# W_dec over two queues, U over 128 rows, FFN's scale and offset on ScalarE: one change to a fused adaptive-norm and FFN kernel

## The reference

```
U = (mu @ W_dec + b_dec).reshape(B, IN_DIM + 1, K)      # B=128, mu 128x64, K=30
weight, bias = split(einsum('bik,kj->bij', U, V))
c = einsum('bsd,bde->bse', x, weight) + bias
gate = c @ Wg.T + bg; top 2 of 8, softmax
x = x + sum over the two of w * (gelu(c @ W1[e].T + b1[e]) @ W2[e].T + b2[e])

h = ln(x, pw_g[id], pw_b[id]); h = ln(h, cp_g[id2], cp_b[id2]); t, s likewise
z = mlp_ln(concat(w0*h, w1*t, w2*m, w3*n, w4*r, w5*s))  # last step: * int_g + int_be
f = silu(z @ w1) * (z @ w2); f = gelu(f @ h1); f = gelu(f @ h2)
x = x + f @ w3
```

## Time and profile before

| | us |
|---|---|
| median of 3 runs | 456.68 |
| lowest and highest | 456.17, 460.87 |
| the profiled execution | 454.07 |
| its span, first to last instruction | 452.2 |
| TensorE busy | 425.7 |
| VectorE busy | 328.6 |
| ScalarE busy | 278.7 |
| GpSimd busy | 141.2 |

### The profile page before, as it was taken

The page is one execution under the profiler, slowest core; times in us unless marked ns, Lnnn a source line. Parts: engine busy times, 40 slices in busy tenths (PEclk is TensorE's granted clock), DMA queues, the critical chain, the costliest instruction groups (busy, mean ns, idle before and its releaser), DMA issues.

```text
span 452.2 us, 5963 instructions
## 1 busy us (share of the span) xinstructions
PE 425.7 (94%) x1897; PEld 283.9 (63%) x1897; DVE 328.6 (73%) x693; ACT 278.7 (62%) x498; POOL 141.2 (31%) x135
## 2 busy tenths in 40 slices
PE   7998898799799999999999999999999999999696
PEld 3875554355366675676667766676577557777495
DVE  3459998699998587686785785887686696755633
ACT  1527836563775677567758665686568446676464
POOL 0013467716454078511011730372127111110000
PEclk9579989999999999999999999999999999999889
DMA  8962348226334027310511260045012400000001
GB/s 235 386 250 93 112 125 256 67 79 204 134 120 144 8 87 227 110 46 13 167 46 46 96 230 6 8 151 166 33 46 77 137 0 2 0 0 25 0 1 50
DMA packets 16847, 45.06 MB, mean 100 GB/s; under 512 B 3209, under 2 KB 5166, under 8 KB 16238
## 3 DMA queue, kind: packets, MB, share of 16 engines
q1 hardware_dynamic: 12240, 31.77, 21.4%
q0 software_dynamic: 3584, 10.49, 7.4%
q10 hardware_dynamic: 991, 2.40, 1.4%
HBM read 40.64 MB, written 4.03 MB: 99 GB/s over the span
## 4 chain that ended last, share of the span: by engine, by line
PE 68%; DVE 5%; ACT 4%; issue 2%; POOL 1%; POOLq 0%; ACTq 0%; DVEq 0%
PE bank L737 20%; PE bank L635 18%; PE bank L683 6%; PE bank L777 5%; PE bank L627 5%; PE bank L722 5%; PE bank L690 2%; PE bank L651 2%; PE bank L766 1%; POOL rstd L1421 1%; DVE bn L1163 1%; DVE mG L1153 1%; PE bank L678 1%; PE bank L696 1%; PE bank L646 1%
## 5 line engine op out<-in xcount | busy, mean ns | idle before, releaser
L635 PE MATMUL bank<-mG,W 128*128 128x512 f32 x256 | 120.8, 599 | 0.5 <-DVE mG L1153 0.5
L882 ACT ACTIVATE mG<-bank,keepP 128x512 f32<-128x512 f32 x128 | 85.9, 683 | 33.7 <-PE bank L627 27.0
L1421 POOL TENSOR_TENSOR rstd<-ve,mhalf 128x4 f32<-128x4 f32 x24 | 34.4, 1434 | 177.9 <-DVE ve L1169 177.1
L1153 DVE TENSOR_TENSOR mG<-mG,gwbs 128x1024 f32<-128x1024 f32 x64 | 78.9, 1240 | 1.9 <-DMA gwbs<-gate_w 1.6
L635 PEld LDWEIGHTS bank<-mG,W 128*128 128x128 f32 x256 | 47.5, 192 | 41.3 <-issue 36.8
L627 PE MATMUL bank<-ts,A 96*128 96x512 f32 x128 | 63.8, 533 | 6.8 <-ACT mG L882 5.0
L943 ACT ACTIVATE G<-bank,keepP 128x512 f32<-128x512 f32 x48 | 32.6, 690 | 26.1 <-PE bank L737 25.9
L1401 POOL DMA_INDIRECT gp<-pgb_in,ixall x32 | 39.9, 1247 | 22.4 <-DVE w_l L1069 11.6
L627 PEld LDWEIGHTS bank<-ts,A 96*128 96x128 f32 x128 | 24.0, 191 | 26.7 <-issue 12.6
L737 PE MATMUL bank<-hA_h,h1w_h 128*128 128x512 f32 x96 | 38.8, 404 | 0.0
L737 PE MATMUL bank<-hB_h,h2w_h 128*128 128x512 f32 x96 | 38.8, 404 | 0.0
(11 more groups left out here) (233 smaller groups left out, 844.8 us busy)
## 6 DMA issues: line engine op xcount, KB each, us to landing
gwbs<-gate_w SPq DMA_DIRECT2D x32, 512.0 KB
outT<-keep SPq DMA_DIRECT2D x7, 256.0 KB, 2.2
...
W1T<-W1T_in SPq DMA_DIRECT2D x1, 1024.0 KB, 10.0
W<-W2T_in SPq DMA_DIRECT2D x1, 1024.0 KB, 13.9
hs<-h1T_in SPq DMA_DIRECT2D x1, 1024.0 KB, 5.9
```

The source lines that it names most:

```text
L635: mm = pe.matmul(OACC[:, :], W2[:, e * HC + c, :], mG[n % NMG][:, c, :], start=False, stop=(e == E - 1 and c == HC - 1))
L882: act.activation(mG[e % NMG][:, c % HC, :], HM[n % 2][:, :], ACT.Gelu, bias=b1c[:, c:c + 1]).then_inc(m_gelu, 1)
L1153: dve.tensor_tensor(mG[n % NMG][:, :, :], mG[n % NMG][:, :, :], gwb[(n // 2) % 2][:, n % 2, :].unsqueeze(1).broadcast_to([P, HC, T]), ALU. ...
L1421: step(pool.tensor_tensor(rstd[:, n, :], ve[:, n, :], mhalf[:, :], ALU.pow))
```

## The change

- W_dec is loaded in two halves of 32 rows, one by SyncE's queue, one by ScalarE's. ScalarE issues all its early loads ahead of its first wait, and runs one tiny copy (`warmA`), so that its table is loaded then. `ld_wd` must reach 64.
- Of the eight pieces of `Wp`, VectorE copies six (0, 1, 2, 4, 6, 7) and ScalarE two (3, 5).
- `Wp` and `muT` have 128 rows. GpSimd clears rows 64 to 127 of the buffer under `Wp`, VectorE rows 64 to 127 of `muT`; row 64 is then filled. The U products, the one for the bias included, run over 128 rows. `WARM` is 5 in place of 6.
- `gap` is 512 values wider and `ct` is moved, so that block 0's gathered table rows (`gp0`) lie in the memory of W1T and `gap` alone, and `tab` of block 0 no longer waits for `small_src`.
- `ff` is a ScalarE instruction with the same scale and offset, and stands in ScalarE's order.
- All five orders are written anew; the FFN weights are split in another order (h2, w3, h1, w12), so that `tab` of block 1, which waits for the rest of w3, needs two of the four rests in place of four. The tables' first rows are shown, the other rows are left out.

```diff
         W1T = sb("W1T", [P, E * H], stack=early)
-        gap = sb("gap", [P, 6144 - KR * (D + 1) - E * H], stack=early)
+        gap = sb("gap", [P, 6656 - KR * (D + 1) - E * H], stack=early)
         VT3 = gap[:, 0:KA]
...
-        muT = sb("muT", [MU + 1, B], stack=early)
+        muT = sb("muT", [P, B], stack=early)
...
-        Wp = hs[0:MU + 1, 0:KR * (D + 1)].rearrange("m (k i) -> m k i", k=KR)
+        Wp = hs[:, 0:KR * (D + 1)].rearrange("m (k i) -> m k i", k=KR)
+        warmA = sb("warmA", [2, P], stack=early)
...
         gcm[0] = sb("gcm0", [P, TT, 3 * P])
-        ct = sb("ct", [P, T])
         gp[0] = sb("gp0", [P, TT, 2 * P])
         norms = sb("norms", [P, 4, TT, P])
         xh, tt, ss, hh = [norms[:, i, :, :] for i in range(4)]
-        cs_, ch = [sb(f"c{k}", [P, T]) for k in "sh"]
+        ct, cs_, ch = [sb(f"c{k}", [P, T]) for k in "tsh"]
...
-        wd_even, wd_odd = sems("wd_even", "wd_odd")
+        wd_dve, wd_act, wp_zero = sems("wd_dve", "wd_act", "wp_zero")
...
-        WARM = 6
+        WARM = 5
+        PIECES = ("v", "v", "v", "a", "v", "a", "v", "v")
...
         def weights_done(eng, *ns):
 
-            eng.wait_ge(w_lo, max((1, 2, 3, 4)[n] for n in ns))
+            eng.wait_ge(w_lo, max((4, 3, 1, 2)[n] for n in ns))
...
             "PE": (
-                (0, "tm0 tm1 gm0 sq0 A0 tm2 A1 tm3 A2 gx0 A3 sq1 tm4 H0 H1 gm1 H2 H3 H4 tm5 H5 H6 gm2 H7 B O0 H8 H9 O1 H10 gm3 sq2 "
-                    "tm6 gm4 H11 H12 O2 sq3 O3 H13 gx1 O4 H14 H15 O5"),
...
+                (0, "tm0 tm1 gm0 A0 A1 tm2 sq0 tm3 gm1 gx0 A2 A3 sq1 H0 H1 tm4 H2 H3 H4 tm5 gm2 H5 H6 tm6 H7 B H8 H9 O0 O1 sq2 gm3 "
+                    "H10 H11 sq3 gm4 O2 H12 gx1 H13 O3 H14 O4 H15"),
...
             "ACT": (
-                (0, "gh tch0 ah0 tch1 ah1 gth0 sza bh ah2 gxh0 gxc0 tch2 ah3 aw g0 g1 wh3 g2 g3 tch3 g4 g5 gth1 ws g6 g7 wh0 tch4 "
-                    "g8 wh1 g9 syc g10 g11 tch5 g12 g13 gxc1 smh0 g14 gxh1 g15"),
...
+                (0, "gh tch0 tch1 bh aw ah0 gth0 ah1 gxh0 sza gxc0 ah2 tch2 ah3 ws g0 g1 g2 g3 smh0 tch3 g4 g5 g6 g7 gth1 g8 tch4 "
+                    "g9 syc g10 g11 tch5 wh2 g12 g13 g14 gxc1 gxh1 smh1 smh2 g15"),
...
             "DVE": (
-                (0, "gl tb0 tb1 am top0 al0 sv0 tb2 gww0 bl al1 sv1 gxl0 tb3 al2 al3 sv3 sv2 top1 q0 gww1 tb4 q1 sv6 sv4 tb5 q2 wl0 "
-                    "q3 q4 tb6 q5 sv5 top2 q6 gxl1 q7 wl1 gww2"),
...
+                (0, "tb0 tb1 gl am top0 al0 gww0 sv0 tb2 tb3 al1 sv1 gxl0 bl al2 sv2 al3 top1 sv6 tb4 sv3 q0 q1 sv4 sml0 q2 tb5 q3 "
+                    "q4 sv5 gww1 top2 q5 gxl1 q6 q7 wl2 sml1 tb6 gww2 x"),
...
             "POOL": (
-                (0, "ix tcl0 tcl1 tcl2 tcl3 srt tcl4 tcl5 tab tcl6 rt0 tcl7 rt1"),
...
+                (0, "tcl0 tcl1 tcl2 srt tcl3 tcl4 tcl5 ix tab rt0 tcl6 rt1 tcl7"),
...
-            load(Wd[0:MU, :], A["W_dec"], ld_wd)
+            load(Wd[0:MU // 2, :], A["W_dec"][0:MU // 2, :], ld_wd)
...
-                if k % 8 == 0:
-                    pe.wait_ge(wd_even, k // 8 + 1)
-                elif k % 8 == 4:
-                    pe.wait_ge(wd_odd, k // 8 + 1)
+                if k % 4 == 0:
+                    who = PIECES[k // 4]
+                    pe.wait_ge(wd_dve if who == "v" else wd_act, PIECES[:k // 4 + 1].count(who))
...
+            def ff(b):
+                act.wait_ge(yT_mm, b + 1)
+                act.activation(flat(YN), XL[:, :], ACT.Identity, scale=igb[:, 0:1], bias=igb[:, 1:2]).then_inc(f_full, 1)
...
+            load(Wd[MU // 2:MU, :], A["W_dec"][MU // 2:MU, :], ld_wd)
             load(muT[0:MU, :], A["cond_512T"], ld_wd)
             load(Wd[MU:MU + 1, :], A["b_dec"], ld_wd)
+            load(Vk[:, :], A["V"], ld_v)
             load(keepP[:, :], A["keepP"], ld_v)
-            load(Vk[:, :], A["V"], ld_v)
-            act.wait_ge(setup0, 1)
-            act.wait_ge(ld_wd, 48)
             load(earlyP[:, :], A["earlyP"], ld_small)
-            wd = Wd[0:MU + 1, :].rearrange("m (i k) -> m k i", k=KR)
-            for q in range(1, 8, 2):
-                act.activation(Wp[:, 4 * q:min(4 * q + 4, KR), :], wd[:, 4 * q:min(4 * q + 4, KR), :], ACT.Copy).then_inc(wd_odd, 1)
             for b in (1, 2):
                 load(keep[b][:, :], A["xT"][:, b * T:(b + 1) * T], x_in[b])
             load(xTr[0][:, :], A["xT"][:, 3 * T:5 * T], ld_x[0])
             load(w12s[:, :], A["w12T"], ld_w[0])
+            act.wait_ge(setup0, 1)
+            act.activation(warmA[:, :], onesf[:, :], ACT.Copy)
+            act.wait_ge(ld_wd, 64)
+            act.wait_ge(wp_zero, 1)
+            wd = Wd[0:MU + 1, :].rearrange("m (i k) -> m k i", k=KR)
+            for q in range(8):
+                if PIECES[q] == "a":
+                    mine = slice(4 * q, min(4 * q + 4, KR))
+                    act.activation(Wp[0:MU + 1, mine, :], wd[:, mine, :], ACT.Copy).then_inc(wd_act, 1)
...
-                dve.wait_ge(w_hi, (2, 3, 4, 1)[n])
+                dve.wait_ge(w_hi, (4, 3, 1, 2)[n])
...
-            def ff(b):
-                dve.wait_ge(yT_mm, b + 1)
-                dve.tensor_scalar(flat(YN), XL[:, :], igb[:, 0:1], igb[:, 1:2], ALU.mult, ALU.add).then_inc(f_full, 1)
...
+            step(dve.memset(muT[MU:P, :], 0.0))
             dve.memset(muT[MU:MU + 1, :], 1.0)
...
-            dve.wait_ge(ld_wd, 48)
-            for q in range(0, 8, 2):
-                dve.tensor_copy(Wp[:, 4 * q:4 * q + 4, :], wd[:, 4 * q:4 * q + 4, :]).then_inc(wd_even, 1)
+            dve.wait_ge(ld_wd, 64)
+            dve.wait_ge(wp_zero, 1)
+            for q in range(8):
+                if PIECES[q] == "v":
+                    mine = slice(4 * q, min(4 * q + 4, KR))
+                    dve.tensor_copy(Wp[0:MU + 1, mine, :], wd[:, mine, :]).then_inc(wd_dve, 1)
...
                     pool.wait_ge(ix_ready, 1)
                     pool.wait_ge(ct_in, 32)
                     pool.wait_ge(a_mm, NC4)
-                    pool.wait_ge(small_src, NSMALL)
...
+            pool.memset(hs[MU:P, :], 0.0).then_inc(wp_zero, 1)
             run(steps, ORDER["POOL"])
```

More of the change, by code:

```diff
@@ L303, in build @@
             "PE": (
[4 rows of a table removed]
[4 rows of a table added]
                     "H15"),
[13 rows of a table removed]
[13 rows of a table added]
             ),
             "ACT": (
[18 rows of a table removed]
[19 rows of a table added]
             ),
             "DVE": (
[15 rows of a table removed]
[16 rows of a table added]
             ),
             "POOL": (
-                (0, "ix tcl0 tcl1 tcl2 tcl3 srt tcl4 tcl5 tab tcl6 rt0 tcl7 rt1"),
+                (0, "tcl0 tcl1 tcl2 srt tcl3 tcl4 tcl5 ix tab rt0 tcl6 rt1 tcl7"),
                 (1, "tab -rt2 rt0 rt1"),
                 (2, "tab rt0 -rt2 rt1"),
-                (3, "tab"),
-                (4, "tab -rt0 =rt2 -rt1 -rt2 rt0 rt1"),
+                (3, "tab rt0 -rt2 rt1"),
+                (4, "tab rt0 -rt2 rt1"),
                 (5, "tab rt0 -rt2 rt1"),
-                (6, "tab rt0 rt1 -rt2"),
-                (7, "tab -rt2 rt0 rt1 rt2"),
+                (6, "tab"),
+                (7, "tab -rt0 =rt2 -rt1 -rt2 rt0 rt1 rt2"),
             ),
             "SP": (
[8 rows of a table removed]
[5 rows of a table added]
+                (5, "gb0 ^stored -li -lx +lt gb1 gb2 gb3 #lt"),
+                (6, "gb0 ^stored -li gb1 -lx lr +lr gb2 gb3 li"),
+                (7, "gb0 ^stored gb1 -lx gb2 gb3 li ~stored lx =stored -sor sop soq"),
             ),
@@ L1016, in _ @@
                      "tc": lambda b: turned_out(b, 0), "sc": lambda b: turned_out(b, 1), "ch": lambda b: turned_out(b, 2),
-                     "zt": zt, "ah": lambda i, n: ah(n), "aw": lambda i: aw_(), "fhi": fhi, "th": th,
+                     "zt": zt, "ah": lambda i, n: ah(n), "aw": lambda i: aw_(), "ff": ff, "fhi": fhi, "th": th,
                      "thr": partial(th_tail, TAIL["r"]), "thp": partial(th_tail, TAIL["p"]), "thq": partial(th_tail, TAIL["q"]),
@@ L1335, in s_m @@
                 dve.tensor_scalar(awx[:, 1:2], awx[:, 0:1], -1.0, None, ALU.mult).then_inc(aw_max, 1)
-            steps = {"q": q_, "x": x1_, "st": st, "t": t_, "s": s_, "hg": hg, "hc": hc, "oh": oh, "a": a, "ff": ff, "flo": flo,
+            steps = {"q": q_, "x": x1_, "st": st, "t": t_, "s": s_, "hg": hg, "hc": hc, "oh": oh, "a": a, "flo": flo,
                      "u": u, "fl": fl, "fo": fo, "ur": partial(u_tail, TAIL["r"]), "up": partial(u_tail, TAIL["p"]), "uq": partial(u_tail, TAIL["q"]),
```

## The result

| | before | after |
|---|---|---|
| median, us (20 runs each) | 457.26 (454.01 to 461.15) | 461.70 (458.33 to 466.51) |
| ratio, 95% interval | | 1.0107 (1.0081 to 1.0132) |
| profiled execution / its span, us | 454.07 / 452.2 | 459.09 / 457.2 |
| granted clock over the span | 0.97 | 0.963 |

The account below looks back on a forecast made before the run. TensorE's own work was taken to bound the body, so gains had to come where it idles or runs slowly, chiefly the start. Terms -6.2 -1.1 -1.0 +0.9 +0.6 +0.3 gave -6.5 us: 450.2 us, range 445 to 457.5.

Parts of the forecast that it names:

- the orders: All engines' rewritten orders: no pair of instructions found that must stall, so 0, with 3 us either way.
- U at full clock: U's multiplications at the start: 128 rows lift the clock from half to full, saving 6.2 us.
- The rival that the clock stays half: Clock stays half through U, by the busyness rule or because zeros count for nothing: 456.2 us, chance 0.18.
- Clock refall: At U's start, one warm-up fewer lengthens the idling, so the clock may fall once more: 0.9 us lost.
- Load: W_dec in two halves: the b_dec transfer that releases VectorE's copy comes 0.6 us later (bounds 1.8 earlier, 3 later).
- Gap: Inside U: TensorE's 1.07 us wait for ScalarE's first piece, behind a table load, goes; 1.1 us saved.
- transforms: First two token transforms after U, at full instead of half clock: 1.0 us saved.
- copies: VectorE's copies out of PSUM around U's end come late after its six pieces: 0.3 us added (bounds 0 and 1.2).
- GpSimd's zeros: GpSimd's clearing of 64 x 4096 at the start: 4.8 us, hidden in the wait until 9.5 us, so nothing.
- a gain lost "in the next stage": Rival: the stage after the head cannot use its gain because of DMA loads; half lost, 453.5 us, chance 0.10.
- Rival (3): ScalarE's new work delays gelu pieces TensorE needs, 5.5 us; with half clock in U too, 461.7 us; chance 0.08.
- idle time after 30 us that grows by more than 3: Sign of a wrong prediction: TensorE's idle time after 30 us growing by more than 3 us.

Follow-up runs that it names:

- head_new: The kernel before with the change's whole preamble (two queues, 128 rows with zeros, six VectorE pieces, early table load): 448.58 us, ratio 0.9844.
- head_65: The kernel before with the new preamble but 65 rows, without the zeros: 457.30 us, ratio 1.0045 against the kernel before.
- rows_ff: The kernel before with only the 128 rows and zeros, plus `ff` on ScalarE ahead of `fhi`: 450.02 us, ratio 0.9891 against the kernel before.
- old_row0: The changed kernel with the first row of each engine's order table as before, the rest new: 448.98 us, ratio 0.9876 against the kernel before.
- row0_others_old: The changed kernel with first rows of ScalarE, VectorE, GpSimd and DMA queue as before, TensorE's new: 461.75 us, no ratio (four runs too far apart).

## Why the prediction was wrong

The terms of the head came out near the forecast. The step that failed is one that the sum put at nothing: the orders.

- **U at full clock, -6.2**: right. The clock was at 1.00 for the whole of U in this execution; 40 multiplications in 4.70 us are 0.118 each (0.122 forecast). The head of the sum, up to the transforms, was -5.5 (the sum without its -1.0); it measured -5.7, here without the refall, and -4.2 in head_new (22.25), with it. As a whole head_new is -7.1 against -6.5 for the sum, with an interval of 3.4 to 10.8.
- **The rival that the clock stays half** fell. head_65 was busy 3.40 of 3.40 us three times over at 0.50; the same products over 128 rows had 1.00, though half of the rows are zeros. The Trainium skill (TensorE: Matmul & The Clock Gate, "What's actually happening") lets the clock go by how busy the engine is; these rows disagree.
- **Clock refall, +0.9**: it did not happen in the profiled execution of the changed kernel (1.00 in the stretch with 0.23 busy us), but in 11 of the 17 kernels with 128 rows, where the transforms start some 1.5 us later for it (22.25 against 20.70). Half of the price was a fair choice.
- **Load, +0.6**: VectorE's copy, which waits for b_dec, began at 11.10, not 9.49: +1.6, inside the bounds, mis-sized by 1.0. 9.49 was itself late; the four other kernels with one queue have 8.32 to 8.51, and the fifteen with two 10.86 to 11.45, so the price by those is 2.4 to 3.1. Whether the split or the one issue more ahead of b_dec costs it was not told apart. ScalarE issues seven more loads ahead of its wait, not ten; that changes nothing, the last is issued by 5.73 us.
- **Gap, transforms, copies**: right; the gap inside U is gone, the transforms gave 1.2 where 1.0 was forecast, the last copy ends 0.64 us after U, as before.
- **GpSimd's zeros**: 3.51 us for 4.8 estimated, hidden. **`ff`**: 774 ns on ScalarE where I took 683 from another line (806 on VectorE), and free as forecast (rows_ff).
- **The orders**: the step that failed reads "I find no pair of instructions in it that must stall ... I give it 0, with 3 us either way". Measured, the tables cost 2.3% (0.9882 to 1.0107), 10 us. Two things were wrong in it. I priced an order by the idle time that was there to be moved, 5.0 us before 150 us; but an order can also add idle time (5.5 us against old_row0), and part of its price is paid in clock, where TensorE is *busy* while it pays (5.0 us; 21.68 of 23.90 us busy at 0.50). And I looked for a single pair that stalls, where what counts is how the sequences fit: none of the mixtures without TensorE's, ScalarE's and VectorE's old rows together got its median under that of the kernel before.
- **The rivals** had a gain lost "in the next stage" at half of it (453.5), for transfers that come too late. The place was right, the mechanism and the size were not: the orders decide it with the same loads, and more than all of the gain goes. Rival (3) had priced a slower kernel at 461.7 us, the very median that was measured. That is luck: it wanted a half clock in U and a cost of `ff` on ScalarE, and neither was there.
- The prediction named what would show it wrong: idle time after 30 us that grows by more than 3. From 30 us to the end it grew by only 1.7 (23.31 against 21.66), though the median came out 11.5 us over the forecast. The sign was blind to the clock row (0.94 to 0.60 from 30 to 60 us), and the idle time of the kernel before hid what its own orders would have saved: old_row0 has 19.25.

Left open: which of the many moves in the new first rows would have to go back. Nor is it shown what a full clock in the stage would give back, since no kernel here had all the new rows and a full clock; row0_others_old suggests that part of it would turn into waiting. The half clock may follow from TensorE being held up as much as it causes it.
